# Local attention: both layers' tiles in one row of steps, gated layers among the tiles of the other sequence, first causal strips prepared beside the last one

## What is computed

```
def _layer(x, wqkv, qs, ksc, wo, lg, lb, w1, b1, w2, b2):       # second block, DEPTH = 2
    h = shift_token(x)                        # second half of the features comes from the token before
    q, k, v = split(h @ wqkv, 3)              # 8 heads of 64
    q = l2norm(q) * qs; k = l2norm(k) * ksc
    q, k = rotary_xpos(q, k)
    o = local_attention(q, k, v)              # windows of 64, each sees itself and the window before
    x = x + o @ wo
    h = layernorm(shift_token(x)) * lg + lb
    a, g = split(h @ w1 + b1, 2)              # hidden 341
    x = x + (a * gelu(g)) @ w2 + b2
    return x

x = layernorm(x + retention(x))               # first block
x = layernorm(x + layer_1(layer_0(x)))        # second block
x = layernorm(x + causal_attention(x))        # third block: 16 heads of 8, keys and queries normed per head
x = layernorm(x + mlp(x))                     # fourth block
```

## Time and profile before

| | |
|---|---|
| median of 3 runs | 1320.1 us |
| lowest, highest | 1303.35, 1336.72 us |
| profiled execution: its own time, its span | 1312.11 us, 1310.4 us |
| TensorE clock granted, mean of the span | 0.855 |
| PE busy, PEld busy | 1034.1 us (79%), 641.6 us (49%) |
| DVE busy | 749.9 us (57%) |
| ACT busy | 537.5 us (41%) |
| POOL busy | 388.2 us (30%) |
| chain that ended last | PE 63%, DVE 19%, issue 7%, ACT 5%, POOL 3% |

### The profile page before, as it was taken

The page is one execution under the profiler, slowest core; times in us unless marked ns, Lnnn a source line. Parts: engine busy times, 40 slices in busy tenths (PEclk is TensorE's granted clock), DMA queues, the critical chain, the costliest instruction groups (busy, mean ns, idle before and its releaser), DMA issues.

```text
span 1310.4 us, 18698 instructions
## 1 busy us (share of the span) xinstructions
PE 1034.1 (79%) x6640; PEld 641.6 (49%) x6640; DVE 749.9 (57%) x1906; ACT 537.5 (41%) x1062; POOL 388.2 (30%) x373
## 2 busy tenths in 40 slices
PE   6996788978883787789579966889788837778994
PEld 3665456646652344344336654566466623434443
DVE  4684678577866644330346755785788666443203
ACT  3730455455533544432046304554455335444320
POOL 2245444144340312200122354441453403123001
PEclk9876799989996678799878867999899966887997
DMA  8000100010000000000100001000100000000001
GB/s 330 2 1 0 26 13 22 1 25 21 14 1 1 1 2 1 1 1 1 32 2 2 1 0 24 15 22 1 25 21 14 1 1 1 2 1 1 1 1 32
DMA packets 11630, 21.61 MB, mean 16 GB/s; under 512 B 1424, under 2 KB 6928, under 8 KB 11024
## 3 DMA queue, kind: packets, MB, share of 16 engines
q1 hardware_dynamic: 11248, 18.60, 4.8%
q10 hardware_dynamic: 288, 1.79, 0.4%
HBM read 11.87 MB, written 1.05 MB: 10 GB/s over the span
## 4 chain that ended last, share of the span: by engine, by line
PE 63%; DVE 19%; issue 7%; ACT 5%; POOL 3%; POOLq 1%; DMA 1%; SPq 0%; DVEq 0%; ACTq 0%
PE bank L731 8%; PE bank L355 7%; PE bank L495 6%; PE bank L389 6%; PE bank L404 5%; PE bank L454 4%; PE bank L658 4%; DVE arena L1102 3%; PE bank L518 2%; PE bank L528 2%; DVE arena L958 2%; PE bank L723 2%; PE bank L644 2%; PE bank L625 2%; PE bank L489 2%
## 5 line engine op out<-in xcount | busy, mean ns | idle before, releaser
L1208 ACT ACTIVATE arena<-bank 128x512 f32<-128x512 f32 (+3 forms) x340 | 164.8, 529 | 262.6 <-PE bank L355 239.6
L355 PE MATMUL bank<-consts_sb,arena 128*128 128x128 f32 x960 | 153.8, 300 | 88.1 <-DVE arena L1094 30.1
L355 PEld LDWEIGHTS bank<-consts_sb,arena 128*128 128x128 f32 x960 | 115.8, 154 | 146.8 <-issue 58.1
L1102 DVE TENSOR_REDUCE arena<-bank 128x2 f32<-128x1024 f32 (+3 forms) x128 | 98.0, 818 | 105.8 <-PE bank L612 105.7
L1495 POOL TENSOR_TENSOR arena<-arena,neghalf 128x16 f32<-128x16 f32 x32 | 93.2, 2914 | 217.2 <-DVE arena L960 217.2
L1460 POOL TENSOR_TENSOR rstd<-vareps,neghalf 128x1 f32<-128x1 f32 x96 | 54.6, 570 | 275.2 <-DVE vareps L788 274.8
L1543 POOL TENSOR_SCALAR_AFFINE_SELECT arena<-arena 128x256 f32<-128x256 f32 x128 | 50.7, 410 | 226.2 <-ACT arena L1384 223.7
L731 PE MATMUL bank<-arena,weights 128*128 128x512 f32 x256 | 110.5, 592 | 0.0
L454 PE MATMUL bank<-weights,x_features 128*128 128x512 f32 x192 | 94.1, 631 | 10.6 <-ACT x_features L1208 10.6
L1384 ACT ACTIVATE arena<-bank 128x1024 f32<-128x1024 f32 (+1 forms) x96 | 81.8, 881 | 48.1 <-PE bank L644 47.6
L389 PE MATMUL bank<-arena 128*128 128x512 f32 x128 | 76.8, 747 | 5.4 <-ACT arena L1232 5.1
(11 more groups left out here) (164 smaller groups left out, 1788.1 us busy)
## 6 DMA issues: line engine op xcount, KB each, us to landing
arena<-arena SPq DMA_DIRECT2D x56, 130.0 KB, 2.3
weights<-wts_dram SPq DMA_DIRECT2D x1, 2824.0 KB, 19.3
weights<-wts_dram SPq DMA_DIRECT2D x1, 1817.0 KB, 13.4
weights<-wts_dram SPq DMA_DIRECT2D x1, 1561.0 KB, 9.5
x_tokens<-x_dram SPq DMA_DIRECT2D x6, 256.0 KB, 3.0
consts_sb<-consts_dram ACTq DMA_DIRECT2D x1, 1232.5 KB, 7.0
out_dram<-x_inner SPq DMA_DIRECT2D x16, 64.0 KB, 1.5
consts_sb<-consts_dram SPq DMA_DIRECT2D x1, 768.0 KB, 4.7
```

Source lines behind the costliest of these rows:

```text
L355: mm = pe.transpose(bank[:, i * P:(i + 1) * P], src, ident)
L1102: ins = dve.tensor_reduce(mx3[:, u % 2, t, 2 * p:2 * p + 2], scores[:, :, at:at + (t + 1) * P], AX, ALU.max)
L1208: return act.activation(dst, src, ACT.Copy)
```

## The change

`window_layer` and `gelu_layer` become one function `window` per engine with 24 steps. `tile_at(s, phase)` gives the tile of a phase: layer 0's tiles begin in steps 0 to 7, layer 1's in steps 11 to 18. The four gated layers are numbered i = 2 l + b. `widen(i)` and its Gelu run inside steps 9, 13 and 20 for i = 0, 1, 2, the `w2` matmuls (`narrow`) in steps 10, 14 and 21, the features of the next sequence or layer in steps 3, 10 and 14, behind the scores and ahead of `oT`. i = 3 comes behind the steps, with the causal projections. `narrow` now writes four tiles into one bank, and DVE adds it with one operation of 512 columns (`block_residual`); POOL's bias is added per sequence (`block_bias`). `gel2` and `hh2` get memory of their own (1.2 thousand more columns), and norm statistics have eight slots instead of four.

The results of sequence 0 are normed at the end of step 21 (`results(0)`), `features3(0)` is in step 22, `project3` in step 23; `results(1)` follows behind the strips. Inside the causal steps, the second sequence's projections and what hangs on them stand one step later.

```
+        FIRST = [0, G + 3]
+        W_STEPS = FIRST[1] + G + 5
+        BEGIN = [FIRST[i // 2] + NT * (i % 2) for i in range(4)]
+        FEATURES_AT = {BEGIN[i] - 1: i for i in range(1, 4)}
+        NORMED_AT = {BEGIN[i] + 9: i for i in range(3)}
+        WIDEN_AT = NORMED_AT
+        NARROW_AT = {BEGIN[i] + 10: i for i in range(3)}
+        GATHER3_AT = BEGIN[2] + 11
+        PROJECT3_AT = BEGIN[2] + 12
-        PROJECT_AT = {0: 4, 1: 5, 2: 6, 3: 7}
+        PROJECT_AT = {1: 4, 2: 5, 3: 6, 4: 7}
```

On PE (`narrow` stands ahead of the transposes of its step; `widen` part 0 between the transposes and the scores, part 1 behind the scores, part 2 behind `oT`):

```
+                def narrow(i, bank=None):
+                    l, b = divmod(i, 2)
+                    bank = take(pe, ("w2", i), [(xf_ready, i + 1)], bank=bank)
+                    pe.wait_ge(hh_ready, 3 * i + 3)
+                    for t in range(NT):
+                        for kb, K in enumerate(KB):
+                            mm = pe.matmul(bank[:, t * P:(t + 1) * P], hh2[0:K, kb, t * P:(t + 1) * P],
...
+                    if s in NARROW_AT:
+                        narrow(NARROW_AT[s])
+                    if s in WIDEN_AT:
+                        widen(WIDEN_AT[s], 0)
...
+                for kb in range(3):
+                    widen(3, kb)
+                narrow(3, bank=7)
```

On DVE, at the end of `window`:

```
+                    if NARROW_AT.get(s) == 2:
+                        results(0)
+                for g in range(NT):
+                    stats3(g)
+                gated_hidden(3, 0)
+                roots()
+                scale(0)
+                gated_hidden(3, 1)
+                scale(1)
+                gated_hidden(3, 2)
+                scale(2)
+                scale(3)
+                for g in range(NT):
+                    low(g)
+                block_residual(3)
+                results(1)
```

On ACT, at the end of `window`:

```
+                act.wait_ge(strips_blank, 2)
+                projected(0)
+                projected(1)
+                normed_features(3)
+                projected(2)
+                gelu(3, 0)
+                projected(3)
+                gelu(3, 1)
+                gelu(3, 2)
```

On POOL, in the steps and behind them:

```
+                    if s in WIDEN_AT:
+                        block_bias(WIDEN_AT[s])
+                    if NARROW_AT.get(s) == 2:
+                        for t in range(NT):
+                            root(NORM["result", t])
+                    if s == GATHER3_AT:
+                        blank_strips()
+                block_bias(3)
+                for t in range(NT):
+                    root(NORM["result", NT + t])
```

668 lines of the change are left out of this document (328 added, 340 removed).

## The result

| | before | changed |
|---|---|---|
| median, executions | 1318.76 us, 20 | 1323.75 us, 20 |
| lowest, highest | 1303.35, 1336.72 us | 1315.2, 1336.54 us |
| ratio changed / before, 95% interval | | 1.0094 (1.0061 to 1.0127) |
| profiled execution, its span | 1312.11, 1310.4 us | 1319.19, 1317.5 us |
| TensorE clock granted, mean | 0.855 | 0.843 |

The changed kernel is slower, by 0.9% as the ratio counts. Two of its executions, of 3336.66 us (one of these 20) and 1950.56 us (in `s5`), were disturbed and are left out from here on. The ratio also leaves out executions more than 1.5% above the fastest of their kernel, and since those of the kernel before scatter more widely it rests on 11 of its 20 and on 18 of the changed kernel's.

A forecast was written before the change was run, and what follows sets the result against it. PE and DVE are nearly full mid-layer, so moved work pays only in PE's holes. Terms sum to +0.55 us a pass, with 1.3 of clock gain -0.75, -1.5 for both: 1310.6 us profiled, 1319 on the median's scale, range 1289 to 1343.

The forecast's parts named there:

- 1 and clock, layer 0 to step 9: Step 4's feature copies made a step earlier, -1.2 us in layer 0; PE's clock perhaps staying up, -1.3 us a pass.
- 2, step 9 to layer 1's q: Between the layers: the other sequence's gated PE work goes elsewhere, 26.7 us becomes 17.8, so -8.9 us.
- 3, first tile of layer 1: Norm and statistics of layer 0's last tiles stand on DVE ahead of what the transposes wait for, +1.75 us.
- 4, steps 13 and 14: Layer 1's full steps take in `widen` and `narrow`: +5.65 us in step 13, +1.65 in step 14.
- rest of layer 1: In step 15 of layer 1 the squares start 0.2 us sooner.
- 5, step 20 to the first causal pass: From layer 1's last tiles through the causal preparation: 49.5 us becomes 50.3, so +0.8 us.
- `results(1)` ahead of the first maxima: At the start of the causal steps `results(1)` keeps DVE 5.4 us, with the features behind it: +1.0 us.
- the first rival: PE's clock stays up, 0.80 instead of 0.74 in the causal steps: 12 to 13 us a pass, 1294; chance 0.2.
- The second rival: Exp late in ACT's queue in steps 13 and 20, cold PE at the tail: +6 a pass and more, 1332; chance 0.2.
- the third: Exp of step 13 late by one table load of 1.28 us a pass, 2.6 in all: 1322; chance 0.1.

The follow-up runs named there:

- s5: The changed kernel repeated without any edit; ratio against the kernel before 1.0136, median 1325.34 us.
- s4: Changed kernel with the causal strips' zeros written by ACT instead of POOL's memsets; ratio against the kernel before 0.9960, 1306.48 us.
- s3: Changed kernel with the second sequence's projections back in causal steps 0 to 3; ratio against the kernel before 0.9957, 1305.57 us.
- s10: Changed kernel with eight DVE copies ahead of `low`, a delay of 2.2 us a pass; ratio against the kernel before 1.0033, 1313.81 us.
- s2: Kernel before with only the second sequence's projections and what hangs on them one causal step later; ratio against the kernel before 0.9976, 1311.4 us.
- s15: Changed kernel with the second sequence's projections one step sooner and 1.1 us of DVE copies ahead of `low`; ratio against before 0.9959, 1305.94 us.
- s7: Changed kernel with the second sequence's projections one step sooner and the strips blanked on ACT; ratio against before 1.0006, 1325.22 us.
- s12: Kernel before with four DVE copies ahead of `low`, 1.1 us a pass; ratio against the kernel before 1.0139, 1326.96 us.
- s8: Changed kernel with `widen` part 0 moved behind the scores, beside part 1; one execution, 1333.36 us.
- s14: Changed kernel with 1.1 us of extra DVE operations at the window stage's start, 275 us ahead of the causal steps; ratio against before 1.0142, 1325.77 us.
- s11: Changed kernel with projections one step sooner, strips blanked on ACT and 1.1 us of DVE copies ahead of `low`; ratio against before 0.9991, 1307.34 us.

## Why the prediction was wrong

The forecast was no change, -0.1%; the time came out 4.8 us above it, inside the range (which is 54 us wide), but slower by more than the uncertainty of the ratio. Step by step, for the first pass, in us:

| term | forecast | measured |
|---|---|---|
| 1 and clock, layer 0 to step 9 | -2.5 | -3.0 |
| 2, step 9 to layer 1's q (26.7 before) | -8.9 | -9.5 |
| 3, first tile of layer 1 | +1.75 | +1.8 |
| 4, steps 13 and 14 (23.0 before) | +7.3 | +9.3 |
| rest of layer 1 | -0.2 | -1.7 |
| 5, step 20 to the first causal pass (49.5 before) | +0.8 | +2.8 |
| `results(1)` ahead of the first maxima | +1.0 | +1.0 |
| causal steps | 0 | +7.3 (with the row above; +0.6 in the second pass) |

**Right:** the change only moves gated work out of one hole into full steps. PE between the layers, in the changed kernel (start us, us, instructions, idle before and what ended it):

```profile
236.38 0.43 PE L512 MATMUL bank<-x_inner,consts_sb 128*128 128x64 f32 x2 [0.28 <-DVE x_inner L1069]
...
246.84 2.90 PE L487 MATMUL bank<-weights,arena 128*128 128x128 f32 x24
250.68 0.63 PE L382 MATMUL bank<-consts_sb,x_inner 128*128 128x128 f32 x4 [0.94 <-DVE x_inner L965]
...
253.60 2.76 PE L505 MATMUL bank<-weights,x_features 128*128 128x512 f32 x6
```

From 236.38 to 253.60 is 17.2 us; forecast 17.8, against 26.7 before. The items that the forecast lists for it add up to 17.45, nearer still. The residual add of 512 columns (L965), taken at 0.75, is 0.69.

**Term 4 was 2.0 us too small,** mostly by the clock. Step 13 was forecast at 15.7 us and took 17.9, step 14 at 14.6 and took 14.4:

```profile
272.49 2.75 PE L505 MATMUL bank<-weights,x_features 128*128 128x512 f32 x6
...
279.50 3.62 PE L478 MATMUL bank<-x_features,weights 128*128 128x512 f32 x4 [2.44 <-DVE arena L1014]
282.91 0.45 PE L541 MATMUL bank<-band_bf,ident_bf 128*128 128x512 bf16 x1
...
285.67 3.70 PE L478 MATMUL bank<-x_features,weights 128*128 128x512 f32 x8
...
290.38 2.85 PE L505 MATMUL bank<-weights,x_features 128*128 128x512 f32 x6
293.07 2.84 PE L487 MATMUL bank<-weights,arena 128*128 128x128 f32 x24
```

`widen` part 0 waits 2.44 us for DVE, as the forecast said it must, and then four matmuls of 512 columns take 3.62 us, twice their price at 2.4 GHz (eight take 3.70 in the same step). So the scores start 10.4 us behind q, k, v where they started 6.5 behind before: 3.9 us later, and the forecast had 2.05. That is 1.9 of the step's 2.2 us. `widen` itself starts 0.5 us later than the scores did, and the scores 3.4 us behind it, where one part was taken at 1.72. ACT in the same step, with both table loads:

```profile
280.34 1.28 ACT L1324 ACT_TABLE_LOAD   x1
...
289.25 1.28 ACT L1387 ACT_TABLE_LOAD   x1
290.54 1.06 ACT L1387 ACTIVATE arena<-arena 128x1024 f32<-128x1024 f32 x1
```

Each load takes 1.28 us, as forecast, and Exp follows at once. The drain of about 1.38 us that the Trainium skill adds (ScalarE: Activation LUTs, What ACT_TABLE_LOAD costs) isn't in these rows: the Gelu ahead ends at 289.2 and Exp starts at 290.54, right behind the load.

**Term 5 was 1.9 too small.** Three of its steps differ, two up and one down. The rows from the end of layer 1 to the projections, POOL, DVE and PE:

```profile
385.39 2.60 POOL L1553 MEMSET arena<- 128x2944 f32 x1
...
389.08 0.74 POOL L1556 MEMSET arena<- 128x768 f32 x1
```

```profile
385.31 4.55 DVE L819 TENSOR_SCALAR arena<-x_inner,meanvar,rstd 128x64 f32<-128x64 f32 x1 [0.67 <-POOL rstd L1505]
385.54 4.36 DVE L819 TENSOR_SCALAR arena<-arena,meanvar,rstd 128x64 f32<-128x64 f32 x1
```

```profile
390.23 5.33 PE L608 MATMUL bank<-weights,x_features 128*128 128x384 f32 x8
395.35 5.49 PE L478 MATMUL bank<-x_features,weights 128*128 128x512 f32 x12
407.02 5.46 PE L487 MATMUL bank<-weights,arena 128*128 128x128 f32 x24 [6.18 <-DVE arena L956]
```

The memsets were done at 389.82, 26.9 us behind step 20 (362.96), forecast 28.3 (its own items, 23.4 and 4.6, make 28.0): the place in the queue was read rightly. But DVE's last norm, 0.3 us elsewhere, hangs until they end at 389.8, and PE's transpose and the projections wait for both. Without the memsets (`s4`) the same two operations took 0.31 each:

```profile
381.05 0.31 DVE L819 TENSOR_SCALAR arena<-x_inner,meanvar,rstd 128x64 f32<-128x64 f32 x1 [0.67 <-POOL rstd L1511]
381.28 0.31 DVE L819 TENSOR_SCALAR arena<-arena,meanvar,rstd 128x64 f32<-128x64 f32 x1
```

The Trainium skill (GPSIMD Engine Reference, Specifications) says that GpSimd shares its SBUF interfaces with VectorE and that the two contend when DVE runs in a 2-port mode or reads two SBUF inputs. The trace agrees that they contend, 4.55 us beside the memsets and 0.31 without (in which mode DVE ran isn't in the rows), and adds that the DVE operation is held until the whole run of memsets has ended. Not every DVE operation is: in the kernel before, the gated product at 382.41, which reads a PSUM bank, took its usual 0.75 us beside a memset of 2.60 us from 381.95. The prediction put 3.1 us a pass on the strips blanked out of the way; it came to 6.0 and 3.6. In the first pass of `s4` the projections start 4.2 us sooner behind layer 1's first q, k, v (132.5 us instead of 136.6), since DVE was freed too; most of the rest is clock: the eight matmuls take 4.02 us instead of 5.33. Then the projections run at 1.2 GHz: eight matmuls in 5.33 us, where the kernel before took 2.85 for its eight, so DVE's last sum ends 8.3 us behind their start where the forecast had 5.6, and `narrow(3)` takes 5.46 instead of 2.7 and holds the strips' transposes by 1.3 us.

**The step that failed** is one that the prediction didn't take. Its sum has no term for the causal steps, so it costed them at what they took before: "against it, that the causal steps' own waits aren't changed", and, of the same steps, "whose queues stay the same". The queues don't: the edit that puts the second sequence's projections one step later has no term and no rival at all, though the diff shows it, and no reason is given for its price of nothing. The runs showed +7.9 us there over both passes of the profiled execution. The table above shows that everything else nearly cancels, as forecast (-0.3 us to the first causal pass, -1.75 forecast), and `s3` shows that undoing this one edit, in the changed kernel, is worth 18 us. It isn't the only way to get the loss back: so do the blanking on ACT (`s4`) and a delay of 2.2 us (`s10`). So the failed step is the causal steps taken as fixed; that the later projections alone cost this is not shown, and `s2` speaks against it. The mechanism is that of the first rival, with the other sign: the clock in the causal steps, 0.74 before over nearly the same stretch, fell to 0.64 in the first pass where the rival asked for 0.80. Half of what the rival named did come: the clock was up when the first pass came (1.00 for 2.44 us ahead of it; before it had been 0.50 for 16.7 us). It fell again 0.98 us later. Its price for the causal steps was nearly right: it put 8.7 us of PE time on a clock of 0.80; in `s3`, at 0.80, PE is busy 102.45 us instead of 110.23 and the stage is 6.4 us shorter than before's 140.0, and 13.7 shorter than the 147.3 at 0.64. What was missing is that this could go both ways, and that two of the prediction's other terms (4 and 5) would show the same effect in small. The prediction did say where it would be wrong: "if the time goes to a place that no term names, the causal steps above all".

The second rival (ACT's queue) and the third (the load in the open) fell as prices, though Exp was late: DVE's last subtraction for it ended at 287.25 and it started at 290.54, behind two Gelus and the load. But it ends 1.2 us behind the start of the next q, k, v (290.38), where the rival needed more than 3 us; the transposes that need it come only at 295.75, behind `narrow`; and step 14 took no longer than forecast. Of the second rival's tail one half came true, `narrow(3)` at 1.2 GHz (5.46 us), and not the other, `widen(3)` (5.49 us for twelve matmuls, near their 5.2).

**A version that beats both.** Earlier projections on the changed kernel: 0.9957 (0.9925 to 0.9990) and with a delay 0.9959 (0.9917 to 1.0000) against before, 22 executions with a mean of 1306.4 us against 1316.6, and a scatter of 2.5 us (standard deviation) instead of 10.2. The ratios alone would not show a gain, since the kernel before against itself gave 1.0045; the means of all executions side by side do (1306.3 against 1316.1 in `s3`, 1306.4 against 1316.2 in `s15`). The blanking on ACT (`s4`) is as fast, 1305.9. The gain of the earlier projections lies in that it was never seen on the slow ways through the causal steps; whether that outlives other changes ahead of them is not known, since the blanking on ACT undid it (`s7`).

## What to carry to other kernels

Where PE runs part of a stage at 1.2 GHz, that stage's time is no constant of the code: before costing a change, note the granted clock of each stage, and give the neighbouring stages a term of both signs, sized by the same work at either clock. When a change of some us a pass moves the time by less than its stages predict, compare the same stage in both passes of one execution first: here 147.3 and 137.0 us from identical instructions pointed at the clock before any experiment. And a move inside idle time needs a term of its own where PE's clock depends on what PE does; try a pure delay as a control before believing any edit of this size.

## What the runs showed of the hardware

- One and the same sequence of instructions in the causal steps of the kernel before took 131.7 and 148.7 us in one execution (`s12`, with 1.1 us of copies ahead of them), at a granted clock of 0.81 and 0.63. In the six profiled passes of the changed kernel only two lengths were seen, 137.0 and 147.2 or 147.3.
- These two lengths go with where the clock last rose: 2.52 or 2.53 us ahead of the first causal pass in the passes of 137.0 us, 2.43 to 2.48 us in those of 147.2 or 147.3 (ten passes of the changed kernel, `s8` and `s14`).
- 1.1 us of additional work on DVE made a kernel faster by 18 us in the median (`s7` 1325.22, `s11` 1307.34; thirteen and four executions) and by 13 in the mean (1321.1, 1307.8).
- 88 additional matmuls a pass lifted the clock from 0.64 (the first pass of the changed kernel) to 0.81 and lowered PE's busy time there from 122.5 to 120.1 us; the stage still grew by 2.1 us.
- A DVE operation of 128x64 from SBUF took 4.55 us beside POOL's memsets and 0.31 without them; one of 85x512 from a PSUM bank took 0.75 beside a memset, as elsewhere.
